# Two-layer convolution block on one core: computed taps in six chunks of eight, paired column halves, VectorE's work spread

## Time and profile before

| | |
|---|---|
| median of 3 runs | 5764.49 us (5759.78 to 5768.80) |
| the profiled execution: its own time | 5764.16 us |
| its span, first to last instruction | 5762.4 us |
| mean granted TensorE clock | 0.833 of full |
| busy: TensorE, VectorE, ScalarE, GpSimd | 4653.8, 4582.5, 2165.7, 4105.2 us |

### The profile page before, as it was taken

How to read it: one execution, slowest core, us unless ns; L and a number is a source line. 1 busy time by engine, 2 the same in 40 slices (tenths; PEclk the granted TensorE clock), 3 DMA queues, 4 the chain that set the end, 5 groups by cost and what they waited for, 6 DMA issues and landing times.

```text
span 5762.4 us, 38546 instructions
## 1 busy us (share of the span) xinstructions
PE 4653.8 (81%) x11780; PEld 1745.7 (30%) x11780; DVE 4582.5 (80%) x5064; ACT 2165.7 (38%) x3057; POOL 4105.2 (71%) x4315
## 2 busy tenths in 40 slices
PE   7576888978879788787887878788897887988783
PEld 3122332323323233232332323233232332323231
DVE  5978969789696886969879697886978979688664
ACT  3333434343343433434434344343433434343320
POOL 1777677776767767677776777767777677776776
PEclk8777888978789787888988889788887888978895
DMA  3334353343534435344343443434334353433433
GB/s 97 106 121 132 99 139 109 117 131 104 142 95 131 122 106 138 94 132 118 111 136 94 132 117 114 134 98 139 109 116 130 97 146 101 129 114 106 123 108 101
DMA packets 281823, 675.11 MB, mean 117 GB/s; under 512 B 77119, under 2 KB 116618, under 8 KB 279370
## 3 DMA queue, kind: packets, MB, share of 16 engines
q0 software_dynamic: 206784, 564.93, 33.2%
q1 hardware_dynamic: 74832, 107.71, 7.4%
HBM read 618.23 MB, written 54.12 MB: 117 GB/s over the span
## 4 chain that ended last, share of the span: by engine, by line
PE 57%; DVE 28%; POOL 6%; issue 5%; ACT 2%; DMA 1%; POOLq 0%; DVEq 0%; ACTq 0%; SPq 0%
PE yo_ps L733 15%; PE z_ps L672 8%; PE conv_ps L630 7%; DVE pairs L1280 6%; DVE conv_ps L1171 6%; POOL gat L493 6%; DVE gat L1301 6%; PE yo_ps L630 5%; PE tap_ps L663 4%; PE z_ps L739 4%; PE conv_ps L553 3%; PE z_ps L671 3%; PE xh_ps L638 2%; DVE stat L1197 1%; DVE xb L1195 1%
## 5 line engine op out<-in xcount | busy, mean ns | idle before, releaser
L493 POOL DMA_INDIRECT gat<-patch_table,ixu x4308 | 4097.2, 951 | 1643.5 <-issue 1268.0
L1301 DVE TENSOR_TENSOR gat<-gat,wgt_ps 128x1024 f32<-128x1024 f32 x1077 | 1305.1, 1214 | 553.4 <-DMA gat<-patch_table,ixu 546.6
L733 PE MATMUL yo_ps<-hat_s,hat_image 128*128 128x512 f32 x3000 | 1398.0, 614 | 8.7 <-DVE hat_wy L1335 8.7
L1280 DVE TENSOR_REDUCE pairs<-gat 128x256 f32<-128x1024 f32 x1024 | 1240.2, 1211 | 0.0
L663 PE MATMUL tap_ps<-ident,pairs 128*128 128x128 f32 x2048 | 398.2, 326 | 838.1 <-DVE pairs L1280 838.1
L973 ACT ACTIVATE val<-tap_ps 128x512 f32<-128x512 f32 x512 | 304.6, 595 | 1439.2 <-PE tap_ps L663 1438.2
L733 PEld LDWEIGHTS yo_ps<-hat_s,hat_image 128*128 128x128 f32 x3000 | 562.5, 196 | 821.2 <-issue 734.5
L672 PE MATMUL z_ps<-val,w_pair 128*64 128x512 f32 x1024 | 668.0, 752 | 13.6 <-ACT val L973 13.6
L663 PEld LDWEIGHTS tap_ps<-ident,pairs 128*128 128x128 f32 x2048 | 262.1, 162 | 1217.9 <-DVE pairs L1280 1033.8
L1171 DVE SCALAR_TENSOR_TENSOR conv_ps<-xh,kb,conv_ps 128x1024 f32<-128x1024 f32 x480 | 617.8, 1287 | 12.7
L1335 DVE TENSOR_TENSOR hat_wy<-yo_ps,hat_wy 128x512 f32<-128x512 f32 x300 | 206.6, 689 | 250.7 <-PE yo_ps L733 248.0
(11 more groups left out here) (219 smaller groups left out, 4304.9 us busy)
## 6 DMA issues: line engine op xcount, KB each, us to landing
gat<-patch_table,ixu POOLq DMA_INDIRECT x4308, 2.7
xb<-in_x SPq DMA_DIRECT2D x31, 1024.0 KB, 9.7
patch_table<-rec SPq DMA_DIRECT2D x120, 256.0 KB, 2.3
hat_image<-patch_table SPq DMA_DIRECT2D x135, 128.0 KB, 4.6
out<-n_z SPq DMA_DIRECT2D x128, 128.0 KB
patch_table<-np SPq DMA_DIRECT2D x2, 1072.5 KB
patch_table<-gat SPq DMA_DIRECT2D x8, 256.0 KB, 2.2
patch_table<-rec SPq DMA_DIRECT2D x16, 97.0 KB
```

Of the source, the lines that this page charges most:

```text
L493: pool.indirect_dma_start(gat[:, k, t * 2 * REC:(t + 1) * 2 * REC], None, table_rows, bass.IndirectOffsetOnAxis(ixu[:, i, k, t:t + 1], 0)) ...
L733: m = pe.matmul(hat_sum[:, :], hat_image[:, i, t, :], hat_s[:, i, :], start=(i == 0), stop=(i == HI - 1))
L1280: dve.tensor_reduce(total, gat[:, k, :].rearrange("p (t x c h) -> p t c x h", t=TILES, x=2, h=2), mybir.AxisListType.XY, ALU.add).then_inc ...
L1301: dve.tensor_tensor(patch, patch, wk.rearrange("p (n h) -> p n h", h=2).unsqueeze(2).to_broadcast([128, TILES * 2, C, 2]), ALU.mult).then_ ...
```

## The change

- **More computed taps.** Chunk 7 gets one in images 1 to 15, and in image 0 chunks 3, 4 and 7 (`HATS`, `HATS0`): 93 in all, where there were 75. Each leaves out the four gathers of tap 8. Image 0's `hat_image` is loaded at the start; for the others the load waits for chunk 7, and so chunk 0 uses the list `PLAN_HAT_LATE`, with its first sum two taps later.
- **Column halves.** Offsets are made for two chunks at a time (`offsets_two`), the one into rows 0 to 40 and the other into rows 64 to 104 of `om_ps`, matmul by matmul in turn. Each product into `z_ps` becomes two of 256 columns, into rows 0 to 63 and 64 to 127 (`to_z`). silu reads both halves.
- **Work off VectorE (images from 1 or 2 on).** The clip becomes relu(20 - y) on ScalarE, and exp takes it as exp(20 - that); `hidden`'s normalising and the lower half of `normalise` go to ScalarE.
- **Work moved.** `x_stats` go from chunks 0 to 3 to chunks 5 and 6; mean, variance and dense layers of image b + 2 from chunk 4 to chunk 7; `normalise` from unit 8 to unit 6 of chunk 4; `points` are made in two halves, in chunks 6 and 7; `hidden` runs at units 6, 7, 8 and at the end of chunk 7. `hat_post 0` comes one tap later.
- **Banks.** `to_pixels` uses `yo_ps`, which the hats' sums use too, so each waits for the other (`ups`, `after_px`).

```diff
-HATS = (0, 1, 2, 3, 4)
-NH = len(HATS)
+HATS0 = (3, 4, 7)
+HATS = (0, 1, 2, 3, 4, 7)
...
-PLAN_NORM = ((1, "project"), (3, "residual"), (4, "x_mean"), (4, "group_mean"), (5, "x_var"), (6, "group_var"), (6, "x_norm"),
-             (7, "hidden_units"), (8, "kernel_taps"), (8, "finish"), (8, "normalise"), (KK, "kernels"))
+PLAN_NORM = ((1, "project"), (3, "residual"), (4, "group_mean"), (5, "group_var"), (6, "normalise"), (8, "finish"))
 PLAN_PREPARE = (
-    ((1, "last_row"), (1, "to_table 0"), (2, "offsets 0"), (3, "to_table 1"), (3, "offsets 1"),
-     (4, "to_table 2"), (5, "to_pixels 0"), (5, "to_table 3"), (6, "offsets 2"),
-     (7, "offsets 3"), (8, "to_table 4"), (8, "finish"), (KK, "to_pixels 1")),
-    ((1, "offsets 4"), (2, "offsets 5"), (2, "to_table 5"), (3, "to_pixels 2"), (4, "offsets 6"), (4, "to_table 6"),
-     (5, "offsets 7"), (6, "to_table 7"), (7, "to_pixels 3"), (8, "finish")),
-    ((1, "points 0"), (2, "points 1"), (2, "next_indices"), (3, "points 2"), (4, "hidden 0"), (5, "hidden 1"),
-     (6, "hidden 2"), (7, "hidden 3"), (8, "finish")),
+    ((1, "last_row"), (1, "offsets 0"), (2, "to_table 0"), (2, "x_stats 0"), (3, "to_table 1"), (4, "offsets 1"), (4, "to_pixels 0"),
+     (5, "to_table 2"), (5, "x_stats 1"), (6, "to_table 3"), (7, "to_pixels 1"), (8, "to_table 4"), (8, "finish")),
+    ((1, "offsets 2"), (2, "to_table 5"), (2, "points 0"), (3, "offsets 3"), (3, "to_pixels 2"), (4, "points 1"), (4, "to_table 6"),
+     (5, "x_stats 2"), (5, "to_table 7"), (6, "points 2"), (6, "to_pixels 3"), (7, "x_stats 3"), (8, "finish")),
+    ((1, "x_mean"), (1, "points 3"), (2, "x_var"), (2, "points 4"), (2, "next_indices"), (3, "x_norm"), (3, "points 5"),
+     (4, "hidden_units"), (5, "kernel_taps"), (6, "kernels"), (6, "hidden 0"), (7, "hidden 1"), (8, "hidden 2"), (8, "finish"), (KK, "hidden 3")),
 )
-PLAN_HAT = ((1, "hat_rows"), (1, "hat_up 0"), (2, "hat_post 0"), (3, "hat_up 1"), (5, "hat_post 1"), (5, "hat_out 0"), (5, "hat_up 2"),
+PLAN_HAT = ((1, "hat_rows"), (1, "hat_up 0"), (3, "hat_post 0"), (3, "hat_up 1"), (5, "hat_post 1"), (5, "hat_out 0"), (5, "hat_up 2"),
             (6, "hat_out 1"), (7, "hat_post 2"), (7, "hat_up 3"), (8, "hat_out 2"), (KK, "hat_post 3"))
+PLAN_HAT_LATE = ((1, "hat_rows"), (3, "hat_up 0"), (4, "hat_post 0"), (5, "hat_up 1"), (6, "hat_post 1"), (6, "hat_out 0"), (7, "hat_up 2"),
+                 (7, "hat_out 1"), (8, "hat_post 2"), (8, "hat_up 3"), (8, "hat_out 2"), (KK, "hat_post 3"))
...
-    return NCH <= q < B * NCH and q % NCH in HATS
+    return q < B * NCH and q % NCH in (HATS if q >= NCH else HATS0)
...
+    own = PLAN_HAT_LATE if g == 0 else PLAN_HAT
+    return by_unit(PLAN_NEXT_HAT[0:1] if has_hat(q + 1) else (), own[0:2] if has_hat(q) else (), plan,
+                   own[2:] if has_hat(q) else (), PLAN_NEXT_HAT[1:] if has_hat(q + 1) else ())
...
-                store_out(b, 5)
+                for g in range(5, NCH - 1):
+                    store_out(b, g)
                 if more:
                     load_hat_image(b + 1)
-                for g in range(6, NCH):
-                    store_out(b, g)
+                store_out(b, NCH - 1)
...
+                if n > 1:
+                    pe.wait_ge(rec_done, n * NCH + 1)
...
+                    if n > 1 and s == 0 and j == 0:
+                        pe.wait_ge(kernel_dve, n * KERNEL_STEPS + 8)
...
+            def offsets_two(n, s):
+
+                if s == 0:
+                    pe.wait_ge(np_done, n * 2 + 2)
+                else:
+                    pe.wait_ge(om_done, n * NCH + s * 2)
+                for i in range(6):
+                    for j in range(2):
+                        m = pe.matmul(om_ps[C * j:C * j + OM, :], w_om[:, i, :], inner(np1, 0, 128, (s * 2 + j) * ROWS + 2 * (i // 3), i % 3),
+                                      start=(i == 0), stop=(i == 5))
+                m.then_inc(om_mm, 2)
...
+                m = pe.matmul(pixel_ps(n)[:, t * PXC:(t + 1) * PXC], cat[rows, tile * 128:(tile + 1) * 128], to_px[rows, :], start=True, stop=True)
...
+                if n > 0 and ups[0]:
+                    pe.wait_ge(hat_scaled, ups[0])
+                if n > 0:
+                    after_px.append(n * NCH + s * 2 + 3)
...
+            def to_z(weights, columns, start=False, stop=False):
+
+                for j in range(2):
+                    m = pe.matmul(z_ps[C * j:C * j + C, 0:CH // 2], weights, columns[:, j * CH // 2:(j + 1) * CH // 2], start=start, stop=stop)
+                return m
...
-                    pe.matmul(z_ps[0:C, :], w_cat[rows, :], cat[rows, span(q % NCH)], start=True, stop=False)
-                pe.matmul(z_ps[0:C, :], w_pair[:, p, :], val[:, p % 2, :], start=False, stop=False)
+                    to_z(w_cat[rows, :], cat[rows, span(q % NCH)], start=True)
+                to_z(w_pair[:, p, :], val[:, p % 2, :])
...
-                    pe.wait_ge(hat_in, q // NCH * HAT_LOADS)
...
+                    pe.wait_ge(hat_in, (q // NCH + 1) * HAT_LOADS)
...
+                if after_px:
+                    pe.wait_ge(px_done, after_px.pop())
+                ups[0] = HT * h + t + 1
...
+                if n > 1:
+                    if s == 0:
+                        act.wait_ge(kernel_dve, n * KERNEL_STEPS + 7)
+                    for j in range(2):
+                        act.wait_ge(xh_mm, n * NCH + s * 2 + (j + 1))
+                        act.activation(n0[C:, j, :], xb[C:, n % 2, span(s * 2 + j)], ACT.Identity, bias=mr0[C:, 2:3],
+                                       scale=mr0[C:, 1:2]).then_inc(n0_done, 1)
...
+                    act.wait_ge(conv_sum, (n - 1) * CONV_SUMS + s * KK + KK)
+                    act.activation(u[:, :, :].rearrange("p j c -> p (j c)"), conv2_ps[:, :], ACT.Relu, bias=twenty, scale=-1.0).then_inc(clip, 2)
                     act.wait_ge(clip, n * NCH + s * 2 + 2)
-                    act.activation(u[:, :, :].rearrange("p j c -> p (j c)"), u[:, :, :].rearrange("p j c -> p (j c)"), ACT.Exp).then_inc(exp_done, 2)
+                    act.activation(u[:, :, :].rearrange("p j c -> p (j c)"), u[:, :, :].rearrange("p j c -> p (j c)"), ACT.Exp, bias=twenty,
+                                   scale=-1.0).then_inc(exp_done, 2)
...
+                if n > 0:
+                    act.activation(np1[0:C, 1:1 + H, 1:1 + W], xb[0:C, n % 2, :].rearrange("p (r w) -> p r w", w=W),
+                                   ACT.Identity, bias=nmean1[0:C, :], scale=rinv1[0:C, :]).then_inc(np_done, 1)
...
-                act.activation(zs[:, :], z_ps[0:C, :], ACT.Silu, bias=bn_shift[:, :], scale=bn_scale[:, :]).then_inc(zs_done, 1)
+                for j in range(2):
+                    m = act.activation(zs[:, j * CH // 2:(j + 1) * CH // 2], z_ps[C * j:C * j + C, 0:CH // 2], ACT.Silu,
+                                       bias=bn_shift[C * j:C * j + C, :], scale=bn_scale[C * j:C * j + C, :])
+                m.then_inc(zs_done, 1)
...
-                if row == 2:
-                    dve.wait_ge(conv_sum, done + KK)
-                    dve.tensor_scalar(uc[:, :, :].rearrange("p j c -> p (j c)"), conv2_ps[:, :], 20.0, None, ALU.min).then_inc(clip, 2)
...
+                if n > 0:
+                    return
...
+                half = part // 3
+                points_of(n, part % 3, math, (n * 2 + half) * MATH_STEPS, half * NCH // 2, NCH // 2)
...
-                    steps["hidden"] = lambda b, g, i: hidden(b + 2, i)
-                    steps["x_stats"] = lambda b, g, i: x_stats(b + 2, g)
+                    steps["x_stats"] = lambda b, g, i: x_stats(b + 2, i)
```

126 lines of the change are left out of this document (69 added, 57 removed).

## The result

The changed kernel takes **5726.57 us**, median of 5 runs (5725.45 to 5734.76), the kernel before 5763.3 beside it: ratio 0.9942, 95% interval 0.9927 to 0.9956. The forecast was 5459 us, and its range ended at 5520. The sign is right, the size is not: 37 us of 304 arrived.

A forecast was written before the change was run, and what follows sets the result against it. GpSimd's gathers were taken to set the time, with 221 us of stalls. Forecast: 119.2 to the first gather + 5319.1 gathers + 13.1 end + 2 + 4 of stalls = 5457 span, + 1.8 = 5459 us; 8-in-10 range 5446 to 5520.

The forecast's parts named there:

- Pace, gathers and end: GpSimd: 4236 gathers at 1.2557 us make 5319.1 us, 90.3 less; after the last gather's issue 13.1 us, plus 2.
- It stays 11 us under 31, so all 221 us of stalls go: GpSimd's stalls begin at distance 31; the forecast reaches 20 after chunk 3, so 221 us go, save 2 and 4.
- the tank: VectorE's lag behind GpSimd's gathers (distance): filled by chunk 7 (16) and chunks 1 to 3 (7 each), overflows in 2 to 4.
- Chunk 7 at 43: Length of chunk 7: 33.8 us of VectorE work, 6 of wait after the third weighing, 3 before the last `finish`.
- Chunk 0 at 42: Length of chunk 0: VectorE busy 36.6 us, 2 to 4 us of wait for the fourth sum, about 42.
- Chunks 1 to 3 at 42: Length of chunks 1 to 3: 47.6 us falls to 42, with 41.1 busy and 1 left of the 2.26 us wait.
- Chunk 6, distance 9 at chunk 7: Chunk 6's VectorE work is 36.3 us against 45.2; the last 4 us stand at its end, so chunk 7 starts at 9.
- A sum at 4.56 us: On TensorE, a computed tap's sum is 5 matmuls, 10 records, and takes 4.56 us.
- Column halves: TensorE's halves were held worth nothing on the path; a rival without their pairing (8%) gave 5459 to 5500 us.
- The load of `hat_image`, 5 us to spare: Load moved to the seam of chunks 7 and 0: lands 12 us after chunk 7's last sum, 5 us to spare.
- stalls remain in part: Rival, 15%: chunk 7 and the seam take 12 us more, the tank overflows in chunks 2 to 4; 5500 to 5570 us.
- Chunk 7 becomes the bound: Rival, 4%: chunk 7's sums run at the lower clock, 8.8 us each, the chunk takes 96 us, the time is 6050.

The follow-up runs named there:

- e1_no7: The change with the computed tap of chunk 7 taken out again (77 computed taps instead of 93): 0.92% less time than the change.
- e7_own7: The change with the computed tap's turns ahead of the next image's kernels and hidden steps in chunk 7: 0.7% less time than the change.
- e11_sel6: The change with chunk 0's turns early, chunk 7's own turns ahead of the hidden steps, chunk 6's selections sooner: 0.9781 of the kernel before.
- e8_post2: The change with VectorE's first product of a computed tap back after the second tap instead of the third: 0.9950 of the kernel before.
- e6_early0: The change with chunk 0's turns put back where the kernel before had them: 2.45% (141 us) less than the change.
- e13_four: The change with each sum made of four of its five matmuls, so the output lacks a part: 3.04% (175 us) less than the change.
- e2_wide_z: The change with the products into z made over 512 columns again: 0.9899 of the kernel before, against 0.9942 for the change.
- e10_no7_wide: The change without chunk 7's computed tap, chunk 0's turns early, z products over 512 columns: 0.9757 of the kernel before, against 0.9643 with z halves.
- e3_fill: The change with four unneeded matmuls ahead of each transposed pair in chunks with a computed tap: 1.0064 of the kernel before, 1.2% slower than the change.

## Why the prediction was wrong, by its steps

- *Pace, gathers and end (4236 x 1.2557, 13.1 + 2):* right. 1.2570, the 90 us did go, and the end took 15.4.
- *VectorE's work:* right to 1.4 us in each of the seven chunks that had a number.
- *"It stays 11 us under 31, so all 221 us of stalls go":* **wrong, this is the step that failed.** The distance at chunk 0 was put at 12 and is 25, after chunk 3 at 20 and is 33, held there by the overflow in chunk 2. The picture of the tank was right: GpSimd waits from some 30 us on, and the stalls follow the largest distance at a chunk's start: 28 to 32 us of stall in the three runs in which it is 30, 62 to 85 where it is 32 to 33, 159 and more from 33.5 on. Once chunk 0 and chunk 7 are relieved (e5_no7_plan) they go, to 30 us. Three of the four lengths put into it were wrong:
  - *Chunk 7 at 43:* 55.5. "VectorE has 5 us of work for some 11" priced the wait for the fourth sum alone, at 6; it is 7.5, and 5.2 ahead of the third, 1.6 ahead of the second and 2.3 ahead of `kb` come to it. The chunk takes 55 us with or without the tap (e1_no7). In e7_own7 and e11_sel6 other waits appear when one is taken away; in e8_post2, where the sums of this chunk take 5.0 us, it falls to 48.9.
  - *Chunk 0 at 42, "2 to 4 us of wait":* 48.4, 11.2 us of wait. (The terms given, 36.6 and 2 to 4, make 39 to 41; "about 42" has a few us of unnamed room in it, and even so is 6 short.) The late list crowds four sums into taps 3 to 8, each behind the one ahead. Worth 141 us (e6_early0).
  - *Chunks 1 to 3 at 42:* 44.9 on average. The 2.26 us ahead of the fourth weighing stayed (2.0), and a wait of about 1 came ahead of the third.
  - *Chunk 6, distance 9 at chunk 7:* right, 9.8.
- *A sum at 4.56 us:* 5.52 on average, mis-sized by 0.96 in 372 sums. The earlier trace rows were read from chunks in which no idle stretch stood ahead of a sum; the change moved sums behind such stretches (6.54 us above) and into chunk 7, where the earlier trace rows had shown a clock of 0.69. The prediction held the lower level for possible in chunk 7 and in the last chunk and priced it in a rival, not in the forecast. Sums shortened by 0.85 us, by leaving work out, give back 175 us (e13_four).
- *Column halves, "neither is on the path":* wrong. The pairing itself is right, and its size too. Groups of the offset matmuls before and after, busy us and mean ns:

```profile
L630 PE MATMUL conv_ps<-np,w_om 128*41 128x512 f32 x732 | 400.2, 705 | 0.0
L630 PE MATMUL yo_ps<-np,w_om 128*41 128x512 f32 x804 | 361.4, 599 | 1.5 <-ACT cat L932 1.5
```
```profile
L648 PE MATMUL conv_ps<-np,w_om 128*41 128x512 f32 x1440 | 399.2, 713 | 48.6 <-ACT cat L997 48.6
```

  (400.2 + 361.4) / 1536 = 0.50 us of TensorE a record, 399.2 / 1440 = 0.28. The products into z fell from 1292 to 794 us in all, though there are more of them. Yet TensorE's work fell by 106 us only, since the sums took 657 us more. And the z halves cost 0.4% in the change (e2_wide_z) and bring 1.1% without the tap of chunk 7 (e10_no7_wide).
- *The load of `hat_image`, 5 us to spare:* right, and more so. Even with the early list TensorE waits for it 25 us in the whole program, so the late list was not needed for the load.
- *The rivals:* "stalls remain in part" (15%) came, in its direction beyond its range: it charged 3 to 8 us an image, and it was 18.7 (images 2 to 13). "Chunk 7 becomes the bound" did not come, and its mechanism was there in part: chunk 7's sums take 5.84 us on average, between the 4.5 of the forecast and the 8.8 of the rival, and the chunk became 55.5 us long, not 96. The granted clock of chunk 7 in image 6 rose from 0.69 to 0.82.

**Faster than both.** e5_no7_plan computes all that the reference asks for in 5563.1 us, 3.6% less than before and 3.0% less than the change: the change, with no computed tap in chunk 7 and chunk 0's turns not moved.

## What to carry to other kernels

An engine that runs ahead until its buffers are full pays for every microsecond that the chain behind it loses between two places where it can catch up. A forecast that empties such a tank should be tested against the sum of small waits, chunk by chunk: here 6 + 12 + 3 x 3 us against 11 of room. VectorE's busy time was right to 4% in each chunk and told little of the lengths: before adding work to a chunk that already waits 20 us, find out on which chain it waits, since the chain need not get shorter when the work does.

One list shared by several chunks can help in some and harm in another by as much: e8_post2 has the time of the change, with chunk 7 shorter by 6.6 us and five others longer. Read an equal time chunk by chunk before calling an edit worthless.

A step moved later to be safe for a load is a cost with a place: price the wait it avoids (2 us here) against what it crowds together (9 us).

## What the runs showed of the hardware

- The same ten records of a sum take from 4.46 to 7.6 us in these traces. Directly behind a pause of over 5 us they took 6.73 on average in the changed kernel and never under 5.95. Short pauses do not make them safe: in chunk 7 above, sums of 6.7 and 7.0 us have 2.08 us of pause ahead and none. A filler of 11 matmuls in such a gap made the next sum short (4.65 for 5.96) and left the two behind it long (6.15 and 5.87).
- The mean granted clock says little of the time: 0.871 with 1.0064 (e3_fill), 0.781 with 0.9643 (e5_no7_plan). In that run, the fastest in which the whole sum is made, TensorE's clock was 0.50 through all of chunk 7 of image 6; VectorE waits there 2.1 us directly for TensorE and 12.4 for gathers (means over images 2 to 13):

```profile
2471.10:2525.10 54.00, 36.09 (x101) 16.16 (x100) 35.09 (x54) 22.18 (x36) 41.18 (x43) 0.50 0.49 129
```

- GpSimd's pace is no constant to four digits: with equal gathers it was between 1.2536 and 1.2598 us from run to run, up to 26 us of a whole time, so that a difference under 0.4% between two single profiles says nothing.
